# A prepared one step less ahead, W2 loaded ahead of x, and the last step reordered in a hypergraph block on one core

## What is computed

```
Hm = (adj != 0);  w = adj[:, 0, :]                  # 64 graphs of 128 nodes
conv(x, W, b) = D^-1 Hm B^-1 Hm^T (x W^T) + b       # D = Hm w, B = column sums of Hm
h   = layer_norm(relu(conv(x, W1, b1)))             # 256 -> 512 features
y   = conv(h, W2, b2) + x                           # 512 -> 256
out = layer_norm(x + y)                             # no scale, no offset
```

## Time and profile before

| what | value |
|---|---|
| runs shown | 315.39 us, median of 3 |
| the profiled execution itself | 318.37 us |
| its span, first to last instruction | 316.6 us |
| PE, weight loads, DVE, ACT, POOL busy | 92%, 83%, 75%, 69%, 42% |
| mean granted TensorE clock | 0.97 of full |
| HBM | 70 GB/s over the span |

### The profile page before, as it was taken

One profiled execution on the slowest core, in us unless ns is written; L12 is line 12 of the kernel. 1 busy time (PEld: TensorE's weight loads), 2 busy tenths in 40 slices (PEclk: granted clock), 3 DMA queues, 4 the chain that ended last, 5 costly groups with the idle time before them and its releaser, 6 DMA issues.

```text
span 316.6 us, 5880 instructions
## 1 busy us (share of the span) xinstructions
PE 291.8 (92%) x1918; PEld 261.4 (83%) x1918; DVE 237.2 (75%) x581; ACT 218.1 (69%) x627; POOL 132.1 (42%) x162
## 2 busy tenths in 40 slices
PE   7677999999999999999999999999999999899381
PEld 6656989899898989898988989898989889797270
DVE  0295559787878889697878787897969787879416
ACT  4469666879687887878796868878787767465400
POOL 2213062635436180917263452708081635444501
PEclk9799899999999999999999999999999999999776
DMA  7911121040412223130404031111212030101011
GB/s 223 294 37 34 34 71 30 10 157 4 131 35 80 88 69 99 66 102 18 151 0 143 24 100 36 66 68 66 69 67 69 5 128 2 66 2 51 18 65 66
DMA packets 26437, 22.55 MB, mean 71 GB/s; under 512 B 860, under 2 KB 26152, under 8 KB 26408
## 3 DMA queue, kind: packets, MB, share of 16 engines
q1 hardware_dynamic: 26304, 22.15, 22.0%
q10 hardware_dynamic: 104, 0.04, 0.0%
HBM read 13.80 MB, written 8.39 MB: 70 GB/s over the span
## 4 chain that ended last, share of the span: by engine, by line
DVE 44%; POOL 27%; issue 12%; PE 8%; ACT 3%; DMA 3%; SPq 1%; DVEq 0%; POOLq 0%
POOL xb_sb L772 11%; POOL rstd L765 7%; DVE g_sb L592 6%; DVE bn_sb L629 6%; DVE pair_sb L607 6%; DVE z_sb L621 6%; DVE r_lo L601 6%; DVE u_lo L564 5%; POOL r_hi L780 5%; POOL rstd L787 5%; DVE q_sb L612 3%; DMA w_raw<-in_L_gnn_W_dram 3%; DVE mv_sb L639 2%; PE bank_v L247 1%; PE bank_g L270 1%
## 5 line engine op out<-in xcount | busy, mean ns | idle before, releaser
L601 DVE TENSOR_TENSOR r_lo<-r_sb,r_hi 128x512 fp32r<-128x512 f32 x64 | 75.6, 1200 | 31.6 <-POOL r_hi L780 31.4
L270 PE MATMUL bank_g<-w_hi,r_hi 128*128 128x258 f32 x256 | 70.6, 307 | 0.0
L787 POOL TENSOR_TENSOR rstd<-var,half_power 128x4 f32<-128x4 f32 (+1 forms) x17 | 17.6, 1037 | 125.5 <-DVE var L643 125.5
L272 PE MATMUL bank_g<-w_lo,r_hi 128*128 128x256 f32 x256 | 65.0, 285 | 0.0
L442 ACT ACTIVATE r_sb<-bank_v,vec 128x512 f32<-128x512 f32 x64 | 44.2, 691 | 24.9 <-PE bank_v L262 24.1
L780 POOL TENSOR_SCALAR r_hi<-r_sb 128x512 fp32r<-128x512 f32 x64 | 46.6, 728 | 25.7 <-ACT r_sb L442 25.6
L262 PE MATMUL bank_v<-u_hi,w_hi 128*128 128x512 f32 x128 | 52.0, 406 | 0.7 <-DVE u_lo L564 0.7
L262 PE MATMUL bank_v<-u_lo,w_hi 128*128 128x512 f32 x128 | 50.6, 395 | 0.0
L262 PE MATMUL bank_v<-u_hi,w_lo 128*128 128x512 f32 x128 | 50.5, 395 | 0.0
L270 PEld LDWEIGHTS bank_g<-w_hi,r_hi 128*128 128x128 f32 x256 | 49.4, 193 | 1.3
L272 PEld LDWEIGHTS bank_g<-w_lo,r_hi 128*128 128x128 f32 x256 | 49.1, 192 | 1.3
(11 more groups left out here) (93 smaller groups left out, 480.6 us busy)
## 6 DMA issues: line engine op xcount, KB each, us to landing
x_sb<-in_x_dram SPq DMA_DIRECT2D x16, 512.0 KB, 3.5
out_dram<-z_sb SPq DMA_DIRECT2D x15, 512.0 KB, 3.0
adj_sb<-in_adj_dram SPq DMA_DIRECT2D x16, 256.0 KB, 4.1
w_raw<-in_L_gnn_W_dram SPq DMA_DIRECT2D x2, 512.0 KB, 6.2
out_dram<-z_sb SPq DMA_DIRECT2D x2, 256.0 KB, 2.2
b_half<-in_L_gnn_b_dram SPq DMA_DIRECT2D x1, 128.0 KB, 7.9
edge_rows<-in_adj_dram ACTq DMA_DIRECT2D x1, 32.0 KB, 3.2
vec_rows<-in_L_gnn_b_dram ACTq DMA_DIRECT2D x1, 2.0 KB
```

The source lines that it names most:

```text
L270: pe.matmul(bank_g[:, n, 0:W2COLS], r_hi[:, i % 2, k, graph(n)], w2_hi[:, k], start=(k == 0), stop=False)
L272: pe.matmul(bank_g[:, n, 0:DOUT], r_hi[:, i % 2, k, graph(n)], w2_lo[:, k], start=False, stop=False, skip_group_check=True)
L601: nc.vector.tensor_tensor(r_lo[:, i % 2, k], r_sb[:, k], r_hi[:, i % 2, k].bitcast(F32), ALU.subtract).then_inc(r_lo_ready, 1)
```

## The change

It does these things:

- SyncE issues the load of W2 ahead of that of x (group 0), and runs six, not seven, adjacency loads ahead.
- Step i now does make_a and make_s of group i + 2 and turn_h of group i + 3. make_s stands behind make_u.
- make_g(i, 3) stands ahead of make_v(i + 1, 1), turn_q and turn_a between g2 and g3.
- The last step does g0, g1, turn_q, g2, g3 and then the residual products.
- On DVE, split_r(i + 1, 3) comes behind make_z(i, 0) (not in step 14), the statistics follow make_z of the same step, make_d follows split_u. For group 0, htb and A are made on DVE.
- On POOL, inverse_std1 comes ahead of the second r_hi chunk; in the last step add_b2 comes ahead of inverse_std2(14), behind the last add_squares.
- On ScalarE, read_ht stands ahead of the third relu, make_htb at the step's end, and normalise(i - 1, 0) ahead of sum_q(i), in the last step too.
- The prologue leaves turn_h(2), turn_h(3) and make_s(2) to step 0 or drops them from it (turn_h(3) is then that of step 0).

```diff
@@ -174,9 +174,9 @@
 
             load_adj(0)
             sp.dma_start(w1_raw[:, :, :], W1.rearrange("(k p) d -> p k d", p=P)).then_inc(weights_in[1], 16)
+            sp.dma_start(w2_raw[:, :, :], W2.rearrange("(k p) h -> p k h", p=P)).then_inc(weights_in[2], 16)
             load_x(0)
             load_adj(1)
-            sp.dma_start(w2_raw[:, :, :], W2.rearrange("(k p) h -> p k h", p=P)).then_inc(weights_in[2], 16)
             load_adj(2)
             load_x(1)
             sp.dma_start(b2_half[:, :], b2.unsqueeze(0).to_broadcast([P, DOUT])).then_inc(weights_in[3], 16)
@@ -184,10 +184,9 @@
             load_x(2)
             load_adj(4)
             load_adj(5)
-            load_adj(6)
             for i in range(G):
-                if i + 7 < G:
-                    load_adj(i + 7)
+                if i + 6 < G:
+                    load_adj(i + 6)
                 if i + 3 < G:
                     load_x(i + 3)
                 if i >= 1:
@@ -201,10 +200,8 @@
         def _(pe):
             def turn_h(j):
                 pe.wait_ge(h_ready, j + 1)
-                if j == 2:
-                    pe.wait_ge(a_ready, 2)
-                elif j:
-                    pe.wait_ge(at_ready, (j + 1) // 2 if j < 4 else j - 1)
+                if j:
+                    pe.wait_ge(at_ready, j)
                 for n in range(PER):
                     mm = pe.transpose(bank_h_bf[:, graph(n)], h_sb[:, j % 2, n], ident_b[:, :])
                 mm.then_inc(h_turned, 1)
@@ -213,10 +210,6 @@
                 pe.wait_ge(htb_ready, j + 1)
                 pe.wait_ge(wcol_ready, j + 1)
                 if j >= 2:
-                    pe.wait_ge(ht_ready, min(j + 2, G))
-                if j == LAST:
-                    pe.wait_ge(at_ready, j)
-                if j >= 3:
                     pe.wait_ge(q_summed, j - 2)
                 else:
                     pe.wait_ge(a_ready, j)
@@ -227,8 +220,6 @@
 
             def turn_a(j):
                 pe.wait_ge(a_ready, j + 1)
-                if j == 1:
-                    pe.wait_ge(ht_ready, 3)
                 for n in range(PER):
                     mm = pe.transpose(bank_h[:, graph(n)], a_sb[:, n], ident[:, :])
                 mm.then_inc(a_turned, 1)
@@ -334,45 +325,50 @@
             pe.transpose(bank_v[:, 0, 0:3 * KH], vec_rows[:, :], ident[0:3 * KH, 0:3 * KH]).then_inc(vec_turned, 1)
             turn_w2()
             turn_a(0)
+            make_u(0)
             turn_h(1)
-            make_u(0)
             pe.wait_ge(w1_ready, 1)
             make_v(0, 0)
-            make_s(1)
             make_v(0, 1)
             sum_w2()
-            turn_h(2)
             make_v(0, 2)
+            make_s(1)
+            make_v(0, 3)
             make_c2()
             turn_a(1)
-            make_v(0, 3)
-            turn_h(3)
-            make_s(2)
 
             pe.wait_ge(w2_ready, 1)
             for i in range(G):
                 last = i == LAST
                 make_g(i, 0)
+                if i == 0:
+                    turn_h(2)
                 if not last:
                     make_u(i + 1)
+                if 0 < i and i + 2 < G:
+                    make_s(i + 2)
                 if i == 0:
                     pe.wait_ge(c2_ready, 1)
                 make_g(i, 1)
-                turn_q(i)
+                if i == 0:
+                    make_s(2)
+                if last:
+                    turn_q(i)
+                else:
+                    make_v(i + 1, 0)
+                make_g(i, 2)
+                if not last:
+                    turn_q(i)
+                if i + 2 < G:
+                    turn_a(i + 2)
+                make_g(i, 3)
                 if last:
                     break
-                if i + 2 < G:
-                    turn_a(i + 2)
-                make_v(i + 1, 0)
-                make_g(i, 2)
                 make_v(i + 1, 1)
-                if i + 4 < G:
-                    turn_h(i + 4)
-                make_g(i, 3)
+                if i + 3 < G:
+                    turn_h(i + 3)
                 make_v(i + 1, 2)
                 make_v(i + 1, 3)
-                if i + 3 < G:
-                    make_s(i + 3)
                 make_y(i, 0)
                 make_y(i, 1)
 
@@ -386,8 +382,6 @@
                 else:
                     pe.wait_ge(q_summed, G)
                 pe.matmul(last_z[n], ident_2[:, :], xb_sb[:, 1, n], start=True, stop=False)
-            make_g(LAST, 2)
-            make_g(LAST, 3)
             for half in range(2):
                 pe.wait_ge(g_ready, LAST * 2 + half + 1)
                 for n in each(half):
@@ -474,61 +468,59 @@
...
-            relu(0, 3)
-            read_ht(3)
-            for k in range(KH):
-                square(0, k)
 
             for i in range(G):
+                if i < LAST:
+                    split_u(i + 1)
                 if i + 2 < G:
                     make_a(i + 2)
+                if i:
+                    normalise(i - 1, 0)
                 if i < LAST:
-                    split_u(i + 1)
-                if i + 3 < G:
-                    make_htb(i + 3)
+                    relu(i + 1, 0)
+                    square(i + 1, 0)
                 sum_q(i)
                 if i + 2 < G:
                     read_at(i + 2)
-                if i < LAST:
-                    relu(i + 1, 0)
-                    square(i + 1, 0)
                 if i:
-                    normalise(i - 1, 0)
+                    normalise(i - 1, 1)
                 if i < LAST:
                     relu(i + 1, 1)
+                    if i + 3 < G:
+                        read_ht(i + 3)
+                    relu(i + 1, 2)
                     square(i + 1, 1)
-                if i + 4 < G:
-                    read_ht(i + 4)
-                if i < LAST:
-                    relu(i + 1, 2)
+                    relu(i + 1, 3)
                     square(i + 1, 2)
-                    relu(i + 1, 3)
                     square(i + 1, 3)
-                if i:
-                    normalise(i - 1, 1)
+                if i + 3 < G:
+                    make_htb(i + 3)
 
         @block.vector
         def _(dve):
@@ -667,64 +659,81 @@
...
             make_h(0)
             make_b(0)
-            make_h(1)
+            make_htb(0)
             make_d(0)
+            make_a(0)
             dve.wait_ge(w1_hi_ready, 1)
             nc.vector.tensor_tensor(w1_lo[:, :, :], bank_g[:, 0:KD], w1_hi[:, :, :].bitcast(F32),
                                     ALU.subtract).then_inc(w1_ready, 1)
-            make_b(1)
-            split_u(0)
             scale_w2(range(KH // 2))
             scale_w2(range(KH // 2, KH))
+            make_h(1)
+            split_u(0)
             dve.wait_ge(w2_scaled, 2)
             nc.vector.tensor_tensor(w2_sum[:, :, :], w2_g[:, 0:2], w2_g[:, 2:4], ALU.add).then_inc(w2_added, 1)
+            make_b(1)
             dve.wait_ge(w2_added, 1)
             nc.vector.tensor_tensor(w2_sum[:, 0], w2_sum[:, 0], w2_sum[:, 1], ALU.add).then_inc(w2_added, 1)
             make_h(2)
-            make_d(1)
             centre_w2()
             split_r(0, 0)
             split_r(0, 1)
+            make_d(1)
             split_w2()
+            split_r(0, 2)
+            split_r(0, 3)
+            read_c2()
+            make_h(3)
             make_b(2)
-            make_h(3)
-            split_r(0, 2)
-            read_c2()
-            split_r(0, 3)
-            make_b(3)
-            make_d(2)
-            add_squares(0)
-            make_h(4)
 
             for i in range(G):
                 if i < LAST:
-                    split_u(i + 1, [0])
-                if i:
-                    take_stats2(i - 1, 0)
+                    split_u(i + 1)
+                if i + 2 < G and i:
+                    make_d(i + 2)
                 if i < LAST:
-                    split_u(i + 1, [1])
-                if i:
-                    take_stats2(i - 1, 1)
-                    make_var2(i - 1)
+                    add_squares(i)
+                if i == 0:
+                    make_d(2)
                 if i == LAST:
                     break
-                if i + 5 < G:
-                    make_h(i + 5)
+                if i + 4 < G:
+                    make_h(i + 4)
+                make_var1(i)
                 split_r(i + 1, 0)
-                make_var1(i)
+                read_g(i)
                 split_r(i + 1, 1)
-                if i + 4 < G:
-                    make_b(i + 4)
-                read_g(i)
+                if i + 3 < G:
+                    make_b(i + 3)
                 split_r(i + 1, 2)
-                split_r(i + 1, 3)
-                make_z(i, 0)
-                if i + 3 < G:
-                    make_d(i + 3)
-                make_z(i, 1)
-                add_squares(i + 1)
+                if i + 1 < LAST:
+                    make_z(i, 0)
+                    split_r(i + 1, 3)
+                    make_z(i, 1)
+                else:
```

(22 more changed lines are left out.)

37 lines of the change are left out of this document (26 added, 11 removed).

## The result

The changed kernel takes **306.48 us** (median of 4 runs, 306.44 to 307.61), beside 315.79 for the kernel before on the same chip (the three runs that gave 315.39, and a fourth: 314.51 to 316.39). The ratio is 0.972, with an interval from 0.968 to 0.976: faster by 9.3 us. The forecast was 310.7, that is 4.7 us faster, with a range from 305.0 to 317.5.

What follows compares the result with a forecast made beforehand. The prediction took TensorE's own work to bound the loop. Start -5.1, deferred work +1.3, loop waits +5.7 and -2.2, last step -4.4 sum to -4.7 us: 310.7 from the 315.4 median, range 305.0 to 317.5 (own range 307.5 to 313.8).

Steps and rivals of the forecast that it cites:

- the first rival: Loop: neither of the two forecast waits, 0.2 us each, is real; total 305.0 us, chance 0.12.
- prologue and step 0: Start: W2 lands earlier and work moves out of the prologue, so step 1 starts near 45.1, not 50.18: -5.1 us.
- deferred work: Steps 1 to 14: one more make_s (1.1) and turn_h (0.2), which the kernel before had done by then: +1.3 us.
- waits in steps 1 to 14: Loop: two new PE waits, 0.4 us a step, +5.7; make_y's waits for g_sb in the last steps go, -2.2.
- last step: Last step: g2 and g3 no longer stand behind the residual products; second read_g starts at +13.5, not +17.9: -4.4 us.
- The wait for relu: Loop, at make_y: its second half waits for relu of the last chunk, 0.2 us a step.
- The wait for the last r_lo: Loop, at g0: the fourth r_lo product waits for r_lo(3), 0.2 us a step.
- r_hi(3) holds r_lo(2) back by 0.35: Loop, DVE and POOL: r_hi(3), from V + 0.97 to V + 1.58, blocks r_lo(2) for 0.35 us; r_lo(3) ends at V + 3.5.
- neither wait is real: Loop: make_y's wait for relu and g0's for r_lo, 0.2 us each, do not occur; 305.0 us, chance 0.12.
- from there all is as before: Last step: from the second read_g to the end takes the same 7.9 us as in the kernel before.
- Half outer gains: Start and last step: rival that the prologue gives 2 us and the last step 3; total 315.2, chance 0.17.
- The slower rival: Loop: it turns from PE to DVE; with 1.0 us a step the total is 319.0, chance 0.18.

Runs made afterwards that it cites:

- experiment 9: The changed kernel with W2's load put back behind adj(1): 306.71 us.
- experiment 2: The kernel before with W2's load ahead of x's, nothing else: 318.41 us, ratio 1.003.
- b_tail_pe: The kernel before with g2 and g3 ahead of the residual products in the last step, on TensorE alone: 312.43 us, ratio 0.982.
- experiment 10: The changed kernel with VectorE's last r_lo of a step moved behind the second z: 311.83 us, ratio 0.986.
- Experiments 3 and 4: The kernel before with g3 ahead of the second v chunk: 319.17 us; also with var1 and inverse_std1 ahead of r_lo and r_hi: 329.05 us.
- experiment 8: The changed kernel with ScalarE's sum_q(15) ahead of normalise(14, 0) in the last step alone: 302.86 us, ratio 0.956.
- a_stats_late: The changed kernel with VectorE's statistics of the second layer norm put back into the next step: 328.89 us.
- a_g3_late: The changed kernel with make_g(i, 3) behind make_v(i + 1, 1) again: 321.87 us, ratio 1.016.

## Why the prediction was right, and where it was not

The forecast was faster by 4.7; it is faster by 9.3. The time of 306.48 lies inside the whole range, down to 305.0, but below the 307.5 of the forecast's own, nearer to the first rival's 305.0. A middle step takes 17.15 us, where I had said 17.65 and named a step that stays at 17.25 as a sign of being wrong. So the direction is right by the start and the last step, and the loop is wrong. Term by term, against the same profiled execution:

| term | forecast | measured |
|---|---|---|
| prologue and step 0 | -5.1 | -5.9 |
| deferred work | +1.3 | about +1.0 |
| waits in steps 1 to 14 | +5.7 - 2.2 | about -3.3 |
| last step | -4.4 | -3.7 |
| sum | -4.7 | -11.9 |

The sum is off by 7.2, the time by 4.2. The difference of 3.0 is the base: the terms are from an execution 3.0 slower than the median that they were subtracted from. That the two errors went against each other is luck. Two slips in the working are small: 14 times 0.4 is 5.6, not 5.7, and the wait of 0.4 for g_sb that I put in step 0 stands at 100.54, in step 3, so that by my own rule -2.6 and not -2.2 belonged in the sum.

**Prologue and step 0: right by its steps.** First g at 25.4 forecast and 24.80 measured, step 1 at 45.1 and 44.25, the wait of turn_q(0) 1.35 and 1.2. W2 landed at 7.6, 1.1 earlier than I let it, and that was worth nothing here: with it late (experiment 9) the time is the same, and early alone (experiment 2) it gives nothing. By the windows, PE's busy time in the prologue falls to 19.15, from 23.74 at a clock of 0.93 and from 21.11 at full clock (b_tail_pe); what waited in it falls too, and step 0 takes 1.6 to 2.6 more. The step that failed is how the term was carried over to the median. I took -5.1 from the profiled execution and subtracted it from 315.4. But 2.9 us of that execution were a start at the lower clock; against a start at full clock the gain is 3.0, and how much of the slow one the median holds is open. I had named the lower clock in step 0 as a bound from below; it belonged in the choice of the base.

**Deferred work: right.** One make_s (0.81 in the middle of a step: 150.73 to 151.54) and one turn_h of 0.2 more.

**Waits in steps 1 to 14: this is the term that was mis-sized, by some 7 us.** Three things in it:

- *The wait for relu*, forecast 0.2, is 0.15: right in kind, over 14 steps 2.1 us instead of 2.8.
- *The wait for the last r_lo*, forecast 0.2, is not there; the r_lo has 0.3 of slack (experiment 10). The step that failed is "r_hi(3) holds r_lo(2) back by 0.35". r_hi(3) starts where I had it, at V + 0.97, but r_lo(2) starts at V + 0.93 and not at V + 1.2: DVE comes to make_b 0.15 earlier, and make_b delays the next r_lo by 0.28 (163.33 to 163.61) where I had taken 0.4. So DVE wins by 0.04 us a race that I had given to POOL, and the last r_lo ends at V + 2.82 instead of V + 3.5. That is 2.8 us of the error. The Trainium skill, in "SBUF — State Buffer", section "Who interferes with whom", says that the one issued second is blocked; the trace agrees, with r_hi's 1.12 in place of 0.62. I had applied the rule in the right place and got the order of issue wrong.
- *A wait in the kernel before that I had read as none.* I wrote that in the middle of the run PE shows no idle time. But make_s there takes 169.55 - 168.44 = 1.11 to the start of make_y, where the same eight products cost 0.81 in the middle of a step (150.73 to 151.54 in the changed kernel). The first half of g_sb is ready at 168.62 + 0.88 = 169.50 in that step, and make_y starts 0.05 later. The row of that weight load names the wait:

```profile
169.55 1.59 PEld L294 LDWEIGHTS bank_v<-g_sb,at_sb 128*128 128x128 f32 x8 [0.25 <-DVE g_sb L592]
```

So make_y waited about 0.3 for g_sb in each of the middle steps (by the weight loads 0.17 to 0.55 in each of the 12 steps in which make_s stands before it), and the changed kernel has no such row. With the order of g3, var1 and the work between g3 and make_y all changed, it is gone: 3 us that my sum did not hold. The rows were there; I used the 1.11 as make_s's cost.

With these, the loop is +1.0 - 2.2 - 3.0 + 2.1 = -2.1, beside the measured -2.3. Experiments 3 and 4 tried to take this wait out of the kernel before by one or two moves, and made it longer; that it goes with the whole order is seen in the rows, not in a run that removes it alone. The rival "neither wait is real" was half right, and the time it gave (305.0) was nearer than my own, but for another reason than the one it stated.

**The last step: right, with two corrections.** The last residual products start at +9.6, behind a sum forecast for +9.7, and the second read_g at +13.3 (forecast +13.5), with sum_q behind normalise as the binding link, as experiment 8 shows by taking it away: -4.1. The "from there all is as before" failed: from there to the end it takes 8.8 us instead of 7.9, because the last products ran at the lower level of the clock (2.08 instead of the 1.13 that they took before).

**Half outer gains** did not occur by the profiled execution, though against a start at full clock the first of them is about 3.0. **The slower rival**, DVE taking over the loop, did not occur either, but it is close: a_stats_late and a_g3_late, each one part of the change undone, turn it to 328.9 and 321.9, both slower than before. The parts of the loop's order are one piece. Their gain over the old order is 2.3 us, but one less step of preparation can't do without them.
